# A decoder layer: the first tile's normalisation, the start's loads and the order of the side work are rewritten

## The reference, cut to what matters

```python
x = x + attn(layernorm(x), Wq, Wk, Wv, Wo)       # 32 query heads, 8 key/value heads of 16, rotary angles, causal
x = x + xattn(layernorm(x), ctx, Wq, bq, Wk, bk) # one head of 512 over 512 context rows; values are ctx itself
x = x + ffn(layernorm(x), w_gate, w_up, w_down)  # weights rounded to -1, 0, 1 times their mean size; gate * up, 1376 wide
def layernorm(x): return (x - mean(x)) / sqrt(var(x) + 1e-5)
```

## Time and profile before

| | us |
|---|---|
| median of 3 executions | 226.63 (226.37 to 226.87) |
| the profiled execution's own time | 226.21 |
| its span in the trace | 224.5 |
| PE busy | 209.5 (93%) |
| DVE / ACT / POOL busy | 146.9 / 124.6 / 65.8 |

### The profile page before, as it was taken

How to read it: one execution, slowest core, us unless ns; L and a number is a source line. 1 busy time by engine, 2 the same in 40 slices (tenths; PEclk the granted TensorE clock), 3 DMA queues, 4 the chain that set the end, 5 groups by cost and what they waited for, 6 DMA issues and landing times.

```text
span 224.5 us, 4343 instructions
## 1 busy us (share of the span) xinstructions
PE 209.5 (93%) x1500; PEld 152.0 (68%) x1500; DVE 146.9 (65%) x556; ACT 124.6 (56%) x210; POOL 65.8 (29%) x87
## 2 busy tenths in 40 slices
PE   8899999999897899998999997999999999999993
PEld 3389878677664675565945445788887877767771
DVE  2488677967889875998424589886645665343333
ACT  2748788777988346197767917357325033323220
POOL 4599917794223383152202212000000010000000
PEclk9999999999999999999999999999999999999999
DMA  6999500024612210649000640000000000020002
GB/s 176 377 402 411 196 1 1 7 72 183 237 65 61 84 49 13 178 134 309 20 4 0 205 170 0 3 0 3 0 0 1 3 0 3 0 93 3 0 0 95
DMA packets 9078, 19.98 MB, mean 89 GB/s; under 512 B 1152, under 2 KB 1536, under 8 KB 9056
## 3 DMA queue, kind: packets, MB, share of 16 engines
q1 hardware_dynamic: 8480, 19.60, 25.2%
q10 hardware_dynamic: 576, 0.10, 0.2%
HBM read 18.58 MB, written 1.05 MB: 87 GB/s over the span
## 4 chain that ended last, share of the span: by engine, by line
PE 77%; DVE 7%; ACT 6%; issue 5%; DMA 3%; SPq 1%; DVEq 0%; POOL 0%; ACTq 0%
PE ps L1376 17%; PE ps L1230 13%; PE ps L1391 8%; PE ps L1267 5%; PE ps L1298 3%; PE ps L1329 3%; PE ps L1210 3%; PE ps L1439 3%; DMA wqkv<-wqkv_dram 3%; PE ps L1164 3%; PE ps L1521 3%; PE ps L1450 2%; PE ps L1480 2%; PE ps L1179 2%; PE ps L1189 2%
## 5 line engine op out<-in xcount | busy, mean ns | idle before, releaser
L1044 DVE CUSTOM_DVE_ANT_0 ps<-ps,maskf 128x128 f32<-128x128 f32 (+1 forms) x128 | 41.2, 394 | 3.4 <-PE ps L1450 2.1
L584 POOL TENSOR_SCALAR_AFFINE_SELECT prob<-prob 128x512 f32<-128x512 f32 x32 | 19.8, 642 | 49.0 <-ACT prob L802 49.0
L802 ACT ACTIVATE prob<-ps 128x1536 f32<-128x1536 f32 x16 | 23.3, 1455 | 19.4 <-PE ps L1486 19.4
L503 POOL TENSOR_TENSOR rstd<-veps,neghalf 128x1 f32<-128x1 f32 x12 | 7.3, 609 | 57.7 <-DVE veps L837 57.7
L672 ACT CAST in_hi<-inter 128x256 f16<-128x256 f32 (+1 forms) x22 | 8.9, 405 | 23.1 <-DVE inter L997 23.1
L1376 PE MATMUL ps<-h_hi,gate_q 128*128 128x256 f16 (+1 forms) x88 | 20.4, 273 | 0.0
L1376 PE MATMUL ps<-h_lo,up_q 128*128 128x256 f16 (+1 forms) x88 | 20.4, 273 | 0.0
L1376 PE MATMUL ps<-h_lo,gate_q 128*128 128x256 f16 (+1 forms) x88 | 20.4, 273 | 0.0
L1376 PE MATMUL ps<-h_hi,up_q 128*128 128x256 f16 (+1 forms) x88 | 20.4, 272 | 0.0
L997 DVE TENSOR_TENSOR inter<-gate_s,ps 128x256 f32<-128x256 f32 (+1 forms) x22 | 9.2, 419 | 15.6 <-PE ps L1376 14.7
L665 ACT ACTIVATE gate_s<-ps 128x256 f32<-128x256 f32 (+1 forms) x22 | 8.4, 384 | 18.8 <-PE ps L1376 18.8
(11 more groups left out here) (189 smaller groups left out, 539.2 us busy)
## 6 DMA issues: line engine op xcount, KB each, us to landing
raw<-gate_dram SPq DMA_DIRECT2D x1, 2752.0 KB, 17.1
raw<-up_dram SPq DMA_DIRECT2D x4, 688.0 KB, 4.1
wqkv<-wqkv_dram SPq DMA_DIRECT2D x4, 384.0 KB, 5.8
raw<-down_dram SPq DMA_DIRECT2D x2, 768.0 KB, 5.2
x<-x_dram SPq DMA_DIRECT2D x4, 256.0 KB, 5.2
xwq<-xwq_dram SPq DMA_DIRECT2D x1, 1024.0 KB, 8.9
xwk<-xwk_dram SPq DMA_DIRECT2D x1, 1024.0 KB, 11.1
wo<-wo_dram SPq DMA_DIRECT2D x1, 1024.0 KB, 18.2
```

The source lines that it names most:

```text
L584: nc.gpsimd.affine_select(out=v, in_=v, compare_op=ALU.is_ge, fill=0.0, base=0, pattern=[[0, GROUP], [1, P]], channel_multiplier=-1).then_ ...
L802: nc.scalar.activation(prob[:, i % 2, :], ps[:, 3:6, :].rearrange("p a b -> p (a b)"), ACT.Exp, scale=DH ** -0.5).then_inc(exp_done, 1)
L1044: nc.vector.tensor_tensor_reduce(scores, scores, mask, 1.0, LOWEST, ALU.add, ALU.max, to).then_inc(max_done, 1)
```

## The change

The statistics of tile 0 no longer end in one scaled tile. DVE subtracts the mean in two halves of 256 columns; PE transposes each half into a bank of its own (`first_T`), ACT copies each; the projection goes row block by row block (`project_first(k)`, both parts e of a k together); the rotation multiplies queries, keys and values of tile 0 by `first_rstd`. The loads are issued from SP and ACT in turn. POOL's order is changed, ACT's transposed tile 1 comes two places earlier, and the tables of the head loop are new. The core of the diff (the new tables are long and cut to the steps that the prediction speaks of):

```diff
-        TILE_BANK = (0, 5, 6, 0)
+        TILE_BANK = (None, 5, 6, 0)
+        FIRST_BANKS = (0, 6)
-        POOL_CHUNKS = [(0, 0), (0, 1), (0, 2), (0, 3), (1, 0), (1, 1), (1, 2), (1, 3), (2, 4)]
+        POOL_CHUNKS = [(0, 0), (0, 1), (0, 2), (0, 3), (1, 0), (1, 1), (1, 2), (1, 3), (2, 1), (2, 4)]
...
-            ([("out", 9), ("max", 12), ("whole", 1, 3), ("n2", 0), ("wo", 1), ("tern", 1, 1)], [("a", 3, 0)],
-             [("tern", 1, 2)]),
-            ([("out", 10), ("max", 13)], [("a", 3, 1), ("n2", 1), ("tern", 1, 3)], [("xT", 1, 0), ("xT", 1, 1),
-             ("high", "wo", 0)]),
-            ([("out", 11), ("max", 14), ("abs", 2, 0), ("abs", 2, 1)], [("g", 0, 0), ("g", 0, 1)], [("abs", 2, 2),
-             ("low", "wo", 0), ("abs", 2, 3)]),
+            ([("out", 9), ("max", 12), ("n2", 0), ("wo", 1)], [("tern", 1, 1), ("a", 3, 0), ("whole", 1, 3)],
+             [("tern", 1, 2), ("tern", 1, 3)]),
+            ([("out", 10), ("max", 13)], [("a", 3, 1), ("n2", 1)], [("xT", 1, 0), ("xT", 1, 1), ("high", "wo", 0)]),
+            ([("abs", 2, 0), ("max", 14), ("abs", 2, 1), ("out", 11)], [("g", 0, 0), ("abs", 2, 2), ("g", 0, 1)],
+             [("abs", 2, 3)]),
...
-        UP_LOADS, CTX_LOAD, DOWN_LOADS = {3: (0, 1), 4: (2,), 5: (3,)}, 6, {10: (0,), 12: (1,), 13: (2, 3)}
+        UP_LOADS, CTX_LOAD, DOWN_LOADS = {3: (0,), 4: (1, 2), 5: (3,)}, 7, {12: (0, 1), 13: (2, 3)}
...
 SP:
-            load_x(0)
-            sp.dma_start(ident[:, :], ident_d).then_inc(ident_in, 16)
-            for k in range(KD):
-                sp.dma_start(wqkv[:, k, :], wqkv_d[k * P:(k + 1) * P, :]).then_inc(wqkv_in[k], 16)
-                if k < 2:
-                    load_x(1 + k)
+            sp.dma_start(x[0:P // 2, 0, :], x_d[0, 0:P // 2, :]).then_inc(x_in[0], 16)
+            sp.dma_start(wqkv[:, 0, :], wqkv_d[0:P, :]).then_inc(wqkv_in[0], 16)
+            load_x(1)
+            sp.dma_start(wqkv[:, 2, :], wqkv_d[2 * P:3 * P, :]).then_inc(wqkv_in[2], 16)
+            load_x(2)
             load_x(3)
+            sp.dma_start(maskf[:, P:2 * P], mask_d).then_inc(const_in, 16)
+            sp.dma_start(bqk[:, 0, :], bq_d).then_inc(const_in, 16)
+            sp.dma_start(bqk[:, 1, :], bk_d).then_inc(const_in, 16)
...
 POOL:
             root(1)
             w_low(0)
+            w_low(1)
             root(2)
-            w_low(1)
+            w_low(2)
             pool.wait_ge(xn_ready, 2)
             root(3)
-            w_low(2)
             w_low(3)
...
 ACT (its four loads at the very start are gone; what follows stands behind `neground`, L762):
-            tile_T(0)
+            act.dma_start(x[P // 2:P, 0, :], x_d[0, P // 2:P, :]).then_inc(x_in[0], 16)
+            act.dma_start(ident[:, :], ident_d).then_inc(ident_in, 16)
+            act.dma_start(wqkv[:, 1, :], wqkv_d[P:2 * P, :]).then_inc(wqkv_in[1], 16)
+            act.dma_start(wqkv[:, 3, :], wqkv_d[3 * P:4 * P, :]).then_inc(wqkv_in[3], 16)
+            act.dma_start(rope[:, :, :, :], rope_d).then_inc(rope_in, 16)
+
+            first_T()
             weights_high(0)
             weights_high(1)
             normalise(1)
             weights_high(2)
+            tile_T(1)
             weights_high(3)
             normalise(2)
-            tile_T(1)
...
 DVE:
             for t in range(TT):
-                dve.wait_ge(x_in[t], 16)
-                stats(t)
+                dve.wait_ge(x_in[t], 32 if t == 0 else 16)
+                moments(t)
+                if t > 0:
+                    variance(t)
                 if t == 0:
-                    normalise(0, lambda: None)
+                    for half, ready in ((0, xn_half), (1, xn_ready)):
+                        cols = slice(half * T, (half + 1) * T)
+                        nc.vector.tensor_scalar(xn[:, 0, cols], x[:, 0, cols], mv[:, 0, 0:1], None,
+                                                ALU.subtract).then_inc(ready, 1)
+                    variance(0)
                 elif t < 3:
                     mean_shift(t)
             tile_low(1)
...
+                def turn(out, heads, angles):
+                    if t == 0:
+                        return nc.vector.scalar_tensor_tensor(out, heads, first_rstd[:, :], angles, ALU.mult, ALU.mult)
+                    return nc.vector.tensor_tensor(out, heads, angles, ALU.mult)
...
 PE:
+            def project_first(k):
+
+                pe.wait_ge(xnT_sb if k >= 2 else xnT_half, 1)
+                pe.wait_ge(wqkv_in[k], 16)
+                for e in range(2):
+                    mm = nc.tensor.matmul(qkv_bank(0, e)[:, 0:QKV - D if e else D], xnT[:, k, 0:P],
+                                          wqkv[:, k, HEAD_COLS[e]], start=(k == 0), stop=(k == KD - 1))
+                    if k == KD - 1:
+                        mm.then_inc(qkv_ps, 1)
...
-            tile_T(0)
-            pe.wait_ge(xnT_sb, 1)
-            project_first(qkv_bank(0, 0), 0).then_inc(qkv_ps, 1)
-            tile_T(1)
-            project_first(qkv_bank(0, 1)[:, 0:QKV - D], 1).then_inc(qkv_ps, 1)
+            first_T()
+            for k in range(KD):
+                if k == 2:
+                    tile_T(1)
+                project_first(k)
             project_high(qkv_bank(1, 0), 1, 0)
```

More of the change, by code:

```diff
@@ L286, in decoder_layer @@
         BESIDE = [
[L287 to L292, removed]
@@ L307, in decoder_layer @@
[L307 to L313, removed]
-        ]
@@ L315, in decoder_layer @@
[L315 to L322, removed]
+            ([("abs", 0, 1)], [("pq", 3), ("rot", 3, 0), ("st", 10)], [("abs", 0, 2)]),
@@ new lines, in decoder_layer @@
+            ([("abs", 0, 3), ("max", 0)], [("rot", 3, 1), ("pk", 3), ("st", 11), ("st", 12)], [("part", 0),
+             ("hi", 3, 0)]),
+            ([("whole", 0, 0), ("max", 1)], [], [("whole", 0, 1), ("a", 0, 0), ("whole", 0, 2)]),
+            ([("max", 2)], [("st", 13), ("tern", 0, 0)], [("a", 0, 1), ("tern", 0, 1), ("lo", 3, 0)]),
+            ([("max", 3), ("out", 0), ("st", 14)], [("hi", 3, 1)], [("a", 1, 0), ("st", 15), ("whole", 0, 3),
+             ("tern", 0, 2)]),
+            ([("out", 1), ("max", 4)], [("st", 16)], [("tern", 0, 3), ("lo", 3, 1), ("a", 1, 1), ("st", 17)]),
@@ new lines, in decoder_layer @@
+            ([("out", 2), ("max", 5)], [("st", 18)], [("abs", 1, 0), ("st", 19), ("abs", 1, 1)]),
+            ([("out", 3), ("max", 6)], [("a", 2, 0)], [("abs", 1, 2)]),
+            ([("max", 7), ("out", 4)], [], [("abs", 1, 3)]),
+            ([("out", 5), ("u", 0), ("max", 8)], [], [("u", 1)]),
+            ([("whole", 1, 0), ("out", 6), ("part", 1), ("whole", 1, 1), ("max", 9)], [], []),
+            ([("out", 7), ("whole", 1, 2), ("c",), ("max", 10)], [("cc", 0)], [("a", 2, 1)]),
+            ([("max", 11), ("cc", 1), ("out", 8)], [], [("wo", 0), ("tern", 1, 0)]),
@@ new lines, in decoder_layer @@
+            ([("out", 9), ("max", 12), ("n2", 0), ("wo", 1)], [("tern", 1, 1), ("a", 3, 0), ("whole", 1, 3)],
[3 more added lines that the diff above has]
+             [("abs", 2, 3)]),
+            ([("max", 15), ("out", 12), ("abs", 2, 4), ("low", "wo", 0), ("xs", 0), ("high", "wo", 1),
+             ("low", "wo", 1)], [("part", 2), ("high", "wo", 2)], [("low", "wo", 2), ("xs", 1), ("xpT", 0)]),
@@ L502, in root @@
                 pool.wait_ge(var_ready, n + 1)
-                nc.gpsimd.tensor_tensor(rstd[:, n % 2:n % 2 + 1], veps[:, n % 2:n % 2 + 1],
+                to = first_rstd[:, :] if n == 0 else rstd[:, n % 2:n % 2 + 1]
+                nc.gpsimd.tensor_tensor(to, veps[:, n % 2:n % 2 + 1],
                                         neghalf[:, :], ALU.pow).then_inc(rstd_ready, 1)
@@ L592, in _, with first_T @@
         def _(act):
-            act.dma_start(rope[:, :, :, :], rope_d).then_inc(const_in, 16)
-            act.dma_start(maskf[:, P:2 * P], mask_d).then_inc(const_in, 16)
-            act.dma_start(bqk[:, 0, :], bq_d).then_inc(const_in, 16)
-            act.dma_start(bqk[:, 1, :], bk_d).then_inc(const_in, 16)
             def tile_T(t):
                 act.wait_ge(xnT_ps, t + 1)
-                nc.scalar.copy((xnT if t == 0 else xnT_r)[:, :, t * P:(t + 1) * P],
+                nc.scalar.copy(xnT_r[:, :, t * P:(t + 1) * P],
                                bank(TILE_BANK[t]).rearrange("p (k q) -> p k q", k=KD)).then_inc(xnT_sb, 1)
+            def first_T():
+                for half, full, done in ((0, xnT_half_ps, xnT_half), (1, xnT_ps, xnT_sb)):
+                    act.wait_ge(full, 1)
+                    nc.scalar.copy(xnT[:, 2 * half:2 * half + 2, 0:P],
+                                   bank(FIRST_BANKS[half], T).rearrange("p (k q) -> p k q", k=2)).then_inc(done, 1)
             def heads_high(t, e):
@@ L837, in stats @@
                 nc.vector.tensor_scalar(veps[:, s:s + 1], mv[:, s, 1:2], EPS, None, ALU.add).then_inc(var_ready, 1)
+            def stats(n):
+                moments(n)
+                variance(n)
             def normalise(n, transposed):
```

65 lines of the change are left out of this document (43 added, 22 removed).

## The result

The changed kernel takes 228.93 us (median of 5 runs, 228.52 to 230.26) against 226.63 for the kernel before (5 runs, 226.37 to 226.93): ratio 1.0106, 95% interval 1.0082 to 1.0129. It is slower, as forecast; the forecast was 228.4. The profiled execution took 229.74 us. Further down, two single executions far from all others (422 us of p3, 532 us of p4) are left out of every median and ratio.

A forecast was written before the change was run, and what follows sets the result against it. PE was taken to bound the kernel: span 224.5 + 1.9 (start) - 0.1 (tables) = 226.3, with 1.71 us around it 228.0, and 0.42 for the median: 228.4 us. Own range 227.2 to 229.6; 80% range 225.8 to 229.7.

The forecast's parts named there:

- What bounds the kernel: PE sets the end; at the start, what counts is when `tile_low(1)` ends, forecast 1.85 us later, 1.9 reaching the loop.
- Loads, x1: At the start, tile 1 of x, sharing engines with ACT's queue, lands between 7.3 and 8.3 us, taken as 7.5; before, 7.06.
- the bound: Worst case for ACT's loads: delayed some 1.5 us by the table load, x0 complete at 5.1, DVE free at 7.1.
- L: The time at which x1, tile 1 of x, lands; taken as 7.5 us, range 7.0 to 8.3.
- ACT's issue behind `neground`: At the start, ACT's loads stand behind this instruction; no delay taken, bounded by all of the table load, 1.28 us.
- First tile at nothing: Tile 0 up to its projection: halved centring and row-block projection gain some tenths of a us, costed at no gain.
- the pause from 12.4 to 15.7: Predicted sign at the start: PE idle about 3 us, waiting for `tile_low(1)`, though w3 landed by 9.5.
- POOL's order, "the step that decides": At the start, `root(2)` behind two `w_low` holds back DVE; `tile_low(1)` ends at L + 8.07, 15.57 against 13.72 us.
- Tables -0.1: Head loop's new placement: `tern(1, 3)` -0.4, `abs(2, 2)` +0.3, the rest 0; sum -0.1 us, bounds -3 and +1.5.
- The clock falls (10%): Rival, chance 0.10: PE's pauses at the start halve its clock behind 15.7 us, costing 1.6 us, 230.0 in all.

The follow-up runs named there:

- p3: The changed kernel with both POOL's order and the start's loads put back to those of before; 227.27 us, ratio 1.0041.
- p4: The changed kernel with DVE's `tile_low(1)` moved ahead of `mean_shift(2)`; 228.56 us, ratio 1.0087.
- p1: The changed kernel with only POOL's order put back to that of before; 228.79 us, ratio 1.0085.
- f1: The kernel before with only the first tile's edits and ACT's earlier cast of tile 1 added; 226.28 us, ratio 0.9980.
- p2: The changed kernel with only the start's loads put back to those of before; 229.10 us, ratio 1.0115.
- t3: The changed kernel with only `tern(1, 3)` put back in step 14 of the head loop; 229.21 us, ratio 1.0121.

## Why the prediction was right, step by step

- **What bounds the kernel**: right. What decides is when `tile_low(1)` ends; the front's loss stays within 0.05 us through groups 4 to 11 of the loop, and it is 1.4 us where 1.9 was forecast.
- **Loads, x1**: right in direction, wrong in what set it. x1 was there when DVE came free at 7.26, without a wait; it was not the limit, x0 was. x0's second half was issued at 1.53 and took 4.1 us, so DVE began at 5.72 where the bound had 5.1. The two errors nearly cancel: L was taken as 7.5 and was 7.26. The rule cited from the Trainium skill ("DMA: Bandwidth & Descriptors", "Issuing engines are not separate DMA queues"), that loads issued by different engines share the same DMA engines, holds here: 327 GB/s in 2.5 to 7.5 us and 382 in 5 to 25, about what one queue moved in the earlier trace rows, 307 and 393.
- **ACT's issue behind `neground`**: no delay was taken, all of the table load was the bound. It was issued at 1.53, 0.74 behind SP's first, while the table load ran until 2.08 and `neground` itself began at 2.09. It waited for the semaphore that `neground` waits for (POOL's three constants, the last written by 1.49), not for its execution.
- **First tile at nothing**: held, but by little. `ident` and x0 came late, the transposes started at 7.16 (5.9 forecast), and tile 0's products ended at 14.52, 0.64 us ahead of `project_high(1)`. Of the pause from 12.4 to 15.7 that I gave as a sign, only this 0.65 us was there: that sign failed, and the first tile was within 0.65 us of being the limit itself. In p1, where `tile_low(1)` ended at 13.46, it was: PE came to `project_high(1)` without a pause. f1 shows that with the old loads this part and ACT's earlier cast gain 0.2%, which I had costed at nothing.
- **POOL's order, "the step that decides"**: right. `root(1)` at L + 1.16, two `w_low` in 3.59 us (3.73 forecast), `root(2)` at L + 5.36, `tile_low(1)` ending at L + 7.76 (8.07 forecast). p2 against p3, and t3 against p1, separate it from the loads. One thing I had not seen: DVE had to wait for x2 until 11.05, where before it was there by 8.98, so `root(2)` could have begun at about 12.15 at the earliest in that execution; the order of POOL decided by half a microsecond only. In p1 x2 was there at 9.88, in t3 at 10.03.
- **Tables -0.1**: wrong, by 1.0 us in the median and 2.3 in the profiled execution. `abs(2, 2)` ahead of the `g(0, 1)` copy was priced at +0.3, "the earlier loads of the down weights giving back most". I had misread the diff: the first of these loads goes from step 10 to step 12, later. Nothing was given back, ACT had 0.25 us of idle time there, and the move cost 0.7 to 0.8; with a late load (p2) it cost 2. `tern(1, 3)` cost the forecast 0.97 at its exponential (0.99 measured), but the 1.35 it was to win did not come: the next thing PE waited for was DVE's `xn`, slowed by POOL's select, which the late exponential had pushed onto it.
- **The clock falls (10%)**: it does, at another place. Near 16 us, where I had put it, the clock reads 1.00 with a pause of 0.65 us. In the changed kernel's trace it falls behind 107 us, after pauses of 0.69 and 0.84; 12 of 33 executions with both new placements show a fall. It costs 0.9 us more of lag in this trace (the changed kernel's 2.20 above its flat part against p1's 1.28; ACT's late copy is hidden by it, PE's wait for `oT` at 116.59 is 0.29 where p1's is 0.86), 1.4 in t3's, and about 1.5 in p3's runs. The Trainium skill's page "TensorE: Matmul & The Clock Gate", "Part 1: The HAM clock gate", says that an idle array falls back to 1.2 GHz. The two levels are those of the rows: the products' distance nearly doubles (0.21 against 0.12 us). But the array was not idle here, it was busy 4.16 of 5 us in that window, so the page's rule by itself does not tell when this fall comes, and the rows do not either.

The median is 0.5 us above the forecast: front -0.5, tables +1.0, and the falls in the slower executions. The direction and the chain that sets the start were forecast; that the number came so near is partly luck, as the two errors have opposite signs, and 0.9 of the 2.3 us come from the tables, which were to win 0.1.
